# Causal filters of a two-layer block: one matrix product per channel instead of four, and block inverses stored along memory

## The reference, cut to what matters

```
fir_short: (4, 64, 5)   fir_long: (4, 64, 64)          # taps of each of 256 channels
short[t, c] = sum_k v[t - (5 - 1 - k), c] * fir_short[c, k]     # zero before the sequence
long[t, c]  = sum_k v[t - (64 - 1 - k), c] * fir_long[c, k]
# delta rule, per head and chunk of 32:
A = where(tri_lo_strict, kb @ k.T, 0)
inv = solve_triangular(eye + A, eye, lower=True, unit_diagonal=True)
```

## Time and profile before

| | |
|---|---|
| Median of three runs (lowest, highest) | 6769.69 us (6754.64, 6771.74) |
| Profiled execution | 6758.43 us, span 6756.7 us |
| TensorE busy, weight loads | 5856.6 us (87%), 4470.5 us (66%) |
| DVE, ACT, POOL busy | 4396.6, 2702.0, 2560.3 us |
| TensorE's mean granted clock | 0.861 of full |
| Filters | about 2741 to 3534 us |
| Inverses | about 3535 to 4282 us |
| Tap matrices loaded | 64 transfers of 384 KB and 64 of 320 KB |

### The profile page before, as it was taken

How to read it: one execution, slowest core, us unless ns; L and a number is a source line. 1 busy time by engine, 2 the same in 40 slices (tenths; PEclk the granted TensorE clock), 3 DMA queues, 4 the chain that set the end, 5 groups by cost and what they waited for, 6 DMA issues and landing times. The chain is left out here.

```text
span 6756.7 us, 139188 instructions
## 1 busy us (share of the span) xinstructions
PE 5856.6 (87%) x43412; PEld 4470.5 (66%) x43412; DVE 4396.6 (65%) x13844; ACT 2702.0 (40%) x6229; POOL 2560.3 (38%) x3710
## 2 busy tenths in 40 slices
PE   6999999999999998699976443599999999999966
PEld 5888888888888887355544332377676776767744
DVE  4777777777777776100005888588777787777840
ACT  2555555555555554100003221144444444444431
POOL 1222222222222222000008664266666666666640
PEclk9999999999999999655555555699999999999978
DMA  1111111111111110355434443122222222222201
GB/s 37 33 33 33 33 38 32 32 33 32 32 32 34 32 39 27 103 137 136 122 97 124 112 112 84 58 61 61 56 60 62 60 62 58 59 61 61 61 21 38
DMA packets 667381, 405.45 MB, mean 60 GB/s; under 512 B 337873, under 2 KB 656658, under 8 KB 666642
## 3 DMA queue, kind: packets, MB, share of 16 engines
q1 hardware_dynamic: 596178, 360.78, 18.7%
q10 hardware_dynamic: 65664, 16.78, 1.2%
q0 software_dynamic: 4800, 18.88, 0.8%
HBM read 258.65 MB, written 137.63 MB: 59 GB/s over the span
## 5 line engine op out<-in xcount | busy, mean ns | idle before, releaser
L509 POOL TENSOR_TENSOR a_shift<-a_mean_var,a_eps 128x2 f32<-128x2 f32 x256 | 71.3, 279 | 1936.2 <-DVE a_mean_var L724 1936.2
L2128 PE MATMUL c_bank<-c_xT,c_gate 128*128 128x512 f32 x1024 | 506.8, 618 | 19.2 <-issue 17.9
L738 DVE SCALAR_TENSOR_TENSOR a_cv<-a_raw,a_taps,a_cv 128x256 f32<-128x256 f32 x1152 | 462.0, 480 | 20.8 <-DVE a_scaled L667 11.0
L810 PE MATMUL a_bank<-a_w,a_hidden 128*128 128x256 f32 x2048 | 459.1, 382 | 0.9 <-ACT a_hidden L598 0.9
L908 PE MATMUL a_bank<-a_turned,a_w 128*128 128x256 f32 x2048 | 454.5, 380 | 1.4 <-ACT a_turned L557 1.1
L1115 DVE COPY b_short<-b_bank 128x512 f32 x64 | 44.1, 691 | 615.6 <-PE b_bank L1092 547.4
L810 PEld LDWEIGHTS a_bank<-a_w,a_hidden 128*128 128x128 f32 x2048 | 383.8, 190 | 71.8 <-issue 20.6
L908 PEld LDWEIGHTS a_bank<-a_turned,a_w 128*128 128x128 f32 x2048 | 384.3, 190 | 54.8 <-ACT a_turned L557 5.2
L1770 POOL TENSOR_TENSOR c_expd<-c_e,c_logit 128x16 f32<-128x16 f32 x128 | 371.7, 2904 | 62.9 <-DVE c_logit L1956 52.5
L1756 POOL TENSOR_TENSOR c_stats<-c_l2sq,half 128x16 f32<-128x16 f32 x128 | 373.5, 2918 | 17.9 <-DVE c_l2sq L1945 17.9
L1328 POOL TENSOR_TENSOR i_coef<-i_base,i_exponent 128x12 f32<-128x12 f32 x128 | 301.1, 2352 | 170.3 <-ACT i_base L1358 101.6
(11 more groups left out here) (297 smaller groups left out, 15151.0 us busy)
## 6 DMA issues: line engine op xcount, KB each, us to landing
b_toeplitz_long<-scratch_filters SPq DMA_DIRECT2D x64, 384.0 KB, 3.7
b_toeplitz_short<-scratch_filters SPq DMA_DIRECT2D x64, 320.0 KB, 4.1
a_x<-in_x SPq DMA_DIRECT2D x64, 256.0 KB, 3.9
scratch_xb<-a_xb SPq DMA_DIRECT2D x64, 256.0 KB, 2.1
scratch_q<-a_qkv_rows SPq DMA_DIRECT2D x64, 256.0 KB, 2.2
scratch_k<-a_qkv_rows SPq DMA_DIRECT2D x64, 256.0 KB, 2.5
scratch_v<-a_qkv_rows SPq DMA_DIRECT2D x64, 256.0 KB, 2.8
b_v_raw<-scratch_v SPq DMA_DIRECT2D x4, 4096.0 KB, 17.8
```

Source lines behind the costliest of these rows:

```text
L738: ins = dve.scalar_tensor_tensor(cv[s][:, n, c], raw[s][:, n, c, j:j + TOK], taps[:, n, c, j:j + 1], cv[s][:, n, c], ALU.mult, ALU.add)
L810: ins = pe.matmul(dst[:, t * D:(t + 1) * D], src[s][:, c, tile_cols(t)], weight[:, c], start=(c == 0), stop=(c == chunks - 1))
L2128: pe.matmul(dst[:].rearrange("p (h t) -> p h t", h=H), gate1[:, c, cols], xT[sl][:, c:c + 1].broadcast_to([P, H, P]), start=(c == 0), stop ...
```

## The change

Filters: a partition now holds a token of a window of 128, of which the first 64 are the 64 tokens before the 64 to be made. So one product of 128 inputs by 128 outputs (64 of the long filter, 64 of the short) makes both filters for 64 tokens. Work goes in eight units, a group of 64 channels and half of the sequences each. `window` is loaded in its later half and its earlier half is copied from there by a second transfer within SBUF. The tap matrices (`matrix`, for a group) are made on TensorE: a shifted identity (`shifted`) times the transposed taps, 64 products of 64 rows per group, alternately on the two halves of the array, and copied by ACT and DVE in turn. There is no flip, no tap matrix is loaded, and nothing is in a loop with registers. Inverses: `below` and `A` are kept transposed (`keep_block` from the causal mask less the identity), so that products and subtractions run along memory in all operands; q, k and xb have eight sets (`LOADS`) instead of four. The planner's shares are others, and one semaphore is shared.

```diff
+    HALF = P // 2
+    WINDOWS = SEQ // HALF
+    PARTS = 2
+    SEQS = batches // PARTS
+    N = SEQS * WINDOWS
+    QUAD = BANK // N
+    K2 = len(KINDS)
+    WIDE = HALF - 1 + P
+    UNITS = [(g, h) for g in range(GROUPS) for h in range(PARTS)]
+    COLUMNS = BANK // (K2 * CH)
+    jobs = [("taps",)]
+    for u, (g, h) in enumerate(UNITS):
+        if u == 0:
+            jobs += [("made", g, n) for n in range(HALF // COLUMNS)]
+        if h == 1 and g + 1 < GROUPS:
+            jobs += [("made", g + 1, n) for n in range(HALF // COLUMNS)]
+        jobs += [("out", u, q) for q in range(CH // QUAD)]
...
+        def _(sp):
+            for n, (name, _) in enumerate(KINDS):
+                size = w["fir_" + name].shape[1]
+                src = w["fir_" + name].rearrange("(c p) k -> p c k", p=P)
+                if n == 0:
+                    sp.wait_ge(taps_made, 1)
+                for twice in range(2):
+                    sp.dma_start(taps[:, :, n, twice, HALF - size:HALF], src).then_inc(taps_in, 16)
+            for u, (g, h) in enumerate(UNITS):
+                if u >= PARTS:
+                    done = last_out[u - PARTS]
+                    sp.wait_ge(bank_full[bank[done]], before[done] + 1)
+                sp.dma_start(window[h][HALF:P], v_v[g, h]).then_inc(v_in[h], 16)
+                sp.wait_ge(v_in[h], 16 * (g + 1))
+                now, prev = (window[h][rows].rearrange("p (b n) c -> p b n c", b=SEQS)
+                             for rows in (slice(HALF, P), slice(0, HALF)))
+                sp.dma_start(prev[:, :, 1:WINDOWS], now[:, :, 0:WINDOWS - 1]).then_inc(window_in[h], 16)
...
+            for u, (g, h) in enumerate(UNITS):
+                for e in ("act", "dve"):
+                    pool.wait_ge(out_made[e], counted(e, "out", u))
+                pool.dma_start(out_v["short"][g, h], out_sb[h][HALF:P]).then_inc(stored["short"][h], 16)
...
+        def take(eng, copy, name):
...
+                elif job[0] == "made":
...
+                    ins = copy(matrix[g % 2][:, :, m * COLUMNS:(m + 1) * COLUMNS],
+                               src[:].rearrange("p (i k c) -> p k i c", k=K2, c=CH))
...
+                else:
+                    _, u, q = job
+                    g, h = UNITS[u]
+                    if g:
+                        for kind, _ in KINDS:
+                            eng.wait_ge(stored[kind][h], 16 * g)
+                    src = opened(job)
+                    ins = copy(out_sb[h][:, :, q * QUAD:(q + 1) * QUAD], src[:].rearrange("p (c n) -> p n c", c=QUAD))
...
+                    if name == "act" and job[2] >= CH // QUAD - 2:
+                        eng.wait_ge(out_made["dve"], counted("dve", "out", u))
+                        eng.dma_start(out_v["long"][g, h], out_sb[h][0:HALF]).then_inc(stored["long"][h], 16)
...
+                    pair = [job, ("made", g, m + 1)]
+                    dst = [opened(j) for j in pair]
+                    for i in range(COLUMNS):
+                        for r in range(2):
+                            rows = slice(r * HALF, (r + 1) * HALF)
+                            at = HALF - 1 - ((m + r) * COLUMNS + i)
+                            ins = pe.matmul(dst[r][:, i * K2 * CH:(i + 1) * K2 * CH].rearrange("p (k c) -> p k c", k=K2),
+                                            shifted[rows, at:at + P], tapsT[rows, :, g * CH:(g + 1) * CH],
+                                            start=True, stop=True)
...
+                    if q == 0:
+                        for e in ("act", "dve"):
+                            pe.wait_ge(matrix_made[e], g + 1)
+                        pe.wait_ge(window_in[h], 16 * (g + 1))
+                    dst = opened(job)
+                    for c in range(q * QUAD, (q + 1) * QUAD):
+                        taps_of = matrix[g % 2][:].rearrange("p k i c -> p (k i) c")[:, :, c]
+                        ins = pe.matmul(dst[:, (c - q * QUAD) * N:(c - q * QUAD + 1) * N], taps_of, window[h][:, :, c],
+                                        start=True, stop=True)
+                    full(ins, job)
...
-    DEPTH = 33.764
+    DEPTH = 33.418
-    SLOTS = 4
+    SLOTS, LOADS = 4, 8
...
-        qk = slots("qk", [P, 2, D])
-        x_b = slots("xb", [P, D])
+        qk = slots("qk", [P, 2, D], LOADS)
+        x_b = slots("xb", [P, D], LOADS)
...
-                    dve.tensor_copy(keep_block[rows], k["keep_below"][rows, rows])
+                    dve.tensor_tensor(keep_block[rows], k["keep_causal"][rows, rows], k["ident"][rows, rows], ALU.subtract)
...
-                        ins = dve.tensor_tensor(T[:, g].rearrange("p c r -> p r c"), unit[:], A[:, g], ALU.subtract)
+                        ins = dve.tensor_tensor(T[:, g], unit[:], A[:, g], ALU.subtract)
...
-                        m[g] = link.mark(dve.tensor_tensor(
-                            part, A[:, g, below_j, j:j + 1].broadcast_to(shape),
-                            T[:, g, 0:j, j:j + 1].rearrange("p c o -> p o c").broadcast_to(shape), ALU.mult))
+                        m[g] = link.mark(dve.tensor_tensor(part[g], A[:, g, j:j + 1, below_j].broadcast_to(shape),
+                                                           T[:, g, 0:j, j:j + 1].broadcast_to(shape), ALU.mult))
...
-                        rest = T[:, g, 0:j, below_j].rearrange("p c r -> p r c")
+                        rest = T[:, g, 0:j, below_j]
```

More of the change, by code:

```diff
@@ L1015, in phase_b @@
-        v_in = sem("v_in")
-        toeplitz_in = [sem(f"toeplitz_in{r}") for r in range(RING)]
-        stored = {n: sem(f"stored_{n}") for n, _, _ in KINDS}
-        waits_met = sem("waits_met")
-        bank_full, bank_read, before = banks.full, banks.read, banks.count
-        block = ctx.enter_context(nc.Block())
-        def flips_of(b):
-            return len(range(b, FLIPS, BANKS))
-        def uses(b, i, g):
-            return i + (min(g + 2, GROUPS) * flips_of(b) + before[b])
-        def flips_before(b, g):
-            return before[b] + g * flips_of(b) + max(g - 1, 0) * TURNS
+        window = [sb(f"window{h}", [P, N, CH]) for h in range(PARTS)]
@@ new lines, in phase_b, with mine, count, counted @@
+        out_made = {e: sem(f"out_made_{e}") for e in ("act", "dve")}
+        stored = {n: [sem(f"stored_{n}{h}") for h in range(PARTS)] for n, _ in KINDS}
+        last_out = {u: ("out", u, CH // QUAD - 1) for u in range(len(UNITS))}
+        last_of = {"act": 0, "dve": 1}
+        def mine(name):
+            return [job for n, job in enumerate(jobs) if n % 2 == last_of[name]]
+        def count(name, *head):
+            return sum(1 for job in mine(name) if job[:len(head)] == head)
+        def counted(name, kind, upto):
+            return sum(1 for job in mine(name) if job[0] == kind and job[1] <= upto)
@@ new lines, in _ @@
+        @block.gpsimd
+        def _(pool):
+            pool.memset(shifted[:], 0.0)
+            for h in range(PARTS):
+                pool.memset(window[h][0:HALF].rearrange("p (b n) c -> p b n c", b=SEQS)[:, :, 0], 0.0)
+            pool.memset(taps[:], 0.0).then_inc(taps_made, 1)
+            pool.wait_ge(taps_made, 1)
+            for twice in range(2):
+                rows = shifted[twice * HALF:(twice + 1) * HALF]
+                ins = pool.affine_select(out=rows, in_=rows, compare_op=ALU.not_equal, fill=1.0, base=-HALF,
+                                         pattern=[[1, WIDE]], channel_multiplier=-1)
+            ins.then_inc(shift_made, 1)
+            for u, (g, h) in enumerate(UNITS):
+                for e in ("act", "dve"):
+                    pool.wait_ge(out_made[e], counted(e, "out", u))
+                pool.dma_start(out_v["short"][g, h], out_sb[h][HALF:P]).then_inc(stored["short"][h], 16)
+            for h in range(PARTS):
+                pool.wait_ge(stored["short"][h], 16 * GROUPS)
@@ L1060, in _ @@
+        @block.scalar
+        def _(act):
+            take(act, lambda dst, src: act.activation(dst, src, ACT.Copy), "act")
+            for h in range(PARTS):
+                act.wait_ge(stored["long"][h], 16 * GROUPS)
+        @block.vector
+        def _(dve):
+            take(dve, dve.tensor_copy, "dve")
         @block.tensor
         def _(pe):
-            def flip(g):
-                pe.wait_ge(v_in, 16 * (g + 1))
-                for n in range(FLIPS):
-                    b = n % BANKS
-                    pe.wait_ge(bank_read[b], flips_before(b, g) + n // BANKS)
-                    ins = pe.matmul(psum[b][:], k["mirror"][:], v_raw[:].rearrange("p n c -> p (n c)")[:, n * BANK:(n + 1) * BANK],
-                                    start=True, stop=True)
-                    ins.then_inc(bank_full[b], 1)
@@ L1118, in store @@
-        def store(eng, name, g):
-            b = plan.bank(RING - 1, name)
-            eng.wait_ge(bank_read[b], uses(b, (g + 1) * TURNS, g))
-            for half in (slice(0, NT // 2), slice(NT // 2, NT)):
-                eng.dma_start(out_v[name][g][:, half], out_sb[name][:, half]).then_inc(stored[name], 16)
```

(20 more changed lines are left out.)

197 lines of the change are left out of this document (78 added, 119 removed).

## The result

The changed kernel takes 6196.95 us (median of four runs, 6195.03 to 6203.81); the kernel before took 6766.45 beside it (6754.64 to 6771.74). The ratio is 0.916, 95% interval 0.915 to 0.918. The profiled execution of the changed kernel took 6197.09 us, its span is 6195.3. The forecast was 6185, so the time lies 12 us above it and inside the range; two stages made it up with errors of opposite sign, and that is what the experiments are about.

What follows compares the result with a forecast made beforehand. TensorE bounds the filter stage, DVE the inverse stage. Filters 28+228+36+10+21=323 us save 471, inverses save 108: 6758.4-471-108=6179, put at 6185 us; range 6120 to 6325.

Steps and rivals of the forecast that it cites:

- The bare load goes with the change of shape: Filter products: weight loads stop lying bare between matmuls once all have one shape; assumed from a rule that tiling changes drain TensorE.
- Products, 228 us: Filter stage: 512 matmuls of 128x128 by 128 columns at 0.445 us each, 228 us; bounds 219 and 374.
- the prediction's own sign: Stated check in the new timeline: products of one unit every 0.43 to 0.46 us if the forecast is right.
- The fifth rival: Filter products: two operands stepping 256 bytes block one another; from 1.59 us each all gain is gone; chance 0.02.
- Window stalls, 10 us: Filter stage: TensorE's waits for window transfers, mostly covered by products and making; 10 us for the last window.
- Making, 36 us: Filter stage: tap matrices made on TensorE, 12 us a group, three groups between products, 36 us.
- the bound from the 256-column row, 8.6: Making one group's tap matrices at full clock: 128 records at 0.067 us, 8.6 us, priced from line L2053.
- Start 28, end 21: Filter stage: 28 us to the first product (load, copy, memsets, taps); 21 us from last copy through final stores.
- the third rival: Filter stage: transfers bind, 64 partitions giving half of 290 GB/s, 43 us a unit, total 6253 us; chance 0.14.
- Inverses, 108 us: Inverse stage: contiguous operands at 1.0 ns an element save 13.5 us a pass, 8 passes, 108 us; bounds 12 and 128.
- The fourth rival: Inverse stage: odd row starts and a repeated operand keep DVE at 1.63 ns; 12 of 108 us left, 6281; chance 0.08.
- Eight sets, nothing: Inverse stage: eight input sets gain nothing, within 0 to 20 us of gain, or 0 to 5 us of loss.

## Why the prediction was right, and where it was not

**What bounds each stage.** Right: TensorE alone in the filter stage, DVE in the inverse stage. The stages that the diff doesn't touch stayed.

**The bare load goes with the change of shape.** Right, and now shown rather than assumed: one shape alone brought 0.44 us in the kernel before, a fixed address brought nothing. The prediction named both as candidates and didn't have to tell them apart, since the change removed both.

**Products, 228 us: mis-sized, 286 measured.** The step that failed is "I take 0.445, near the stream, since both things that could hold the load back are gone". The five rows of before that made the formula all had weights along memory; the load of 0.107 us in it is the price of that form. The change turned the weights into an operand with a step, which the prediction saw ("No row has weights that step 64 floats") and gave the price of the nearest rows. The same trace had the price of a stepped read, in the stream: 0.213 us a record against 0.11. Put on the load it gives two reads of 0.21 in parallel, and that these then take 0.28 together couldn't be read from any row of before. By the prediction's own sign, a product every 0.43 to 0.46 us, this step was wrong. The fifth rival, reads that block one another, was right in kind and far off in size: 0.56, not 1.59.

**Window stalls, 10 us: measured 0, but for the wrong reason.** The sum of transfers was good, 34 us a unit foreseen (29 at 290 GB/s and 5 of latency) and 33.2 measured where they bind (at 250 GB/s). The longer products (two units 71.7 us) covered them. With products of 0.44 the waits were 20 us, twice what the forecast put there. With the weights along memory the stage took 317 us, where the sum said 323: 10 us more of waits and 14 less of making nearly cancel.

**Making, 36 us: 22 measured**, 7.34 us a group instead of 12. It ran at full clock at 0.057 us a record; the bound from the 256-column row, 8.6, was nearer than the value taken between the two clocks.

**Start 28, end 21: 26.8 and 22.2 measured.** The two transfers took 12.8 and 11.8 us. A transfer that touches 64 partitions and runs alone moved 204 to 206 GB/s, not half of the 290 of the earlier trace rows, which is the end of the third rival. The Trainium skill's 196 GB/s for 64 partitions ("SBUF — State Buffer", Door 1) was the nearer figure. These rows are of the changed kernel: the first load (its first microsecond went at 284, the last six at 205), the copy of the earlier half, and the second load:

```profile
2743.00:2751.00 8.00, 7.65 (x94) 7.68 (x96) 3.32 (x5) 3.15 (x6) 0.00 (x0) 0.67 1.30 215
2755.00:2762.00 7.00, 0.00 (x0) 0.00 (x0) 0.00 (x0) 0.00 (x0) 0.00 (x0) 0.51 0.97 204
2766.00:2773.00 7.00, 7.00 (x26) 7.00 (x26) 1.38 (x2) 0.60 (x1) 0.00 (x0) 0.80 1.30 206
```

**Inverses, 108 us: 123 measured.** The round of 240 elements is 1.40 us, as said, and one of 58 elements 0.64 (3714.18 to 3714.82): (1.40-0.64)/728 = 1.04 ns an element, where 1.0 was taken. Alone the pass gained 14.1 us (49.3 to 35.2) where 13.5 was taken. In a turn, among DVE's other work, it gained 15: the stepped operations had been slower there (465 and 489 ns in the mean, 437 and 438 alone) than the ones along memory now are (340 and 345, 328 and 324 alone). The price was taken from the last pass, where DVE runs alone, and used for turns in which it doesn't. The fourth rival fell: the repeated operand didn't hold DVE at 1.63 ns.

**Eight sets, nothing: held**, at most a few us.

**The sum.** 26.8 + 286 + 22 + 0 + 22 = 357 (the stage took 357.8), 35 above the forecast's 323; inverses 15 better than it. 6758.4 - 436 - 123 = 6199, against 6197; the stages ahead were 3 us shorter. That the forecast came within 12 us is in part luck: the 35 us too few in the filter stage were offset by 15 in the inverse stage, 3 ahead of both, and the 6 that the forecast had put on its sum. The mechanism was right but for the read of the weights.

## What to carry to other kernels

When a change swaps which way an operand lies, price that operand's read by a row that has the same step, whichever operand the row has it in; that the slower read sets the pace held here with at most one operand stepping (0.22 us a record with one, 0.113 with none), and not with both (0.28). Then ask what the next limit is at the price you expect and at a worse one: here the stalls were hidden by the very error in the products. And a transfer within SBUF on a full queue can be replaced by copies on engines that are idle most of the time; a layout whose weights lie along memory cost its copies 0.34 to 0.47 us more each, and no time.

## What the runs showed of the hardware

- TensorE, two records of 128 columns at full clock: 0.227 us with both operands along memory, 0.44 with weights or stream stepping 256 bytes, 0.56 with both; with a step of 8 bytes 0.23 to 0.24.
- Products whose shape changes from one to the next (128x128, 128x64, 128x128, 128x32) went at a granted clock of 0.50 with TensorE busy 150 us of 150 and its weight loads 87; the same kernel with the narrow ones made full went at 1.00, with TensorE busy 50 us of 50 and its weight loads 46. The prediction had not asked what the shapes do to the clock; which property of the products moves it is open.
- DVE and ACT copy from partitions 64 to 127 to partitions 0 to 63 at 0.66 and 0.99 us for 960 floats, 0.68 and 1.03 ns each.
- Transfers of 64 partitions: 204 to 206 GB/s for one alone, 248 GB/s for several at once.
